# A graph-attention and message-passing kernel: the first four edge groups take keys and values from gathered rows of x, the query table is made first, and table stores and six loads go out on ScalarE's queue

## The reference

```python
q = (x @ Wq.T + bq).reshape(N, H, C)          # N=3125, H=4, C=32
k = (x @ Wk.T + bk).reshape(N, H, C)
v = (x @ Wv.T + bv).reshape(N, H, C)
alpha = jnp.sum(q[dst] * k[src], axis=-1) / np.sqrt(C)
m = jax.ops.segment_max(alpha, dst, num_segments=N)
e = jnp.exp(alpha - m[dst])
z = jax.ops.segment_sum(e, dst, num_segments=N)
msg = (e / z[dst])[:, :, None] * v[src]
out = jax.ops.segment_sum(msg, dst, num_segments=N)
conv = out.reshape(N, H * C) + x @ Wskip.T + bskip
# then: Wout, layer norm, a 512-wide MLP, layer norm: the new node features
# then the second layer: gather of node features by src, a small MLP over the
# edge weights, products with edge directions, segment_sum by dst, W_out, layer norm
```

## Time and profile before

| | us |
|---|---|
| runs (3) | 2982.51, 2999.38, 3002.67; median 2999.38 |
| the profiled execution | 2992.43 |
| its span, first to last instruction | 2990.6 |
| mean granted TensorE clock | 0.728 of full speed |

### The profile page before, as it was taken

One profiled execution on the slowest core, in us unless ns is written; L12 is line 12 of the kernel. 1 busy time (PEld: TensorE's weight loads), 2 busy tenths in 40 slices (PEclk: granted clock), 3 DMA queues, 4 the chain that ended last, 5 costly groups with the idle time before them and its releaser, 6 DMA issues. The chain is left out here.

```text
span 2990.6 us, 37370 instructions
## 1 busy us (share of the span) xinstructions
PE 1866.1 (62%) x9706; PEld 1438.2 (48%) x9706; DVE 1725.1 (58%) x4970; ACT 1264.9 (42%) x3058; POOL 1582.4 (53%) x1617
## 2 busy tenths in 40 slices
PE   3255554554554554545558167877788778777887
PEld 3154443453443444444545045555555555555565
DVE  2454565554554554554666056666666666666678
ACT  0244454554554554544545033433334334333344
POOL 4345555555555555555202756666666666666640
PEclk7556666666666666666678578888887888788889
DMA  7455554544554554544301211111111111111110
GB/s 220 131 144 160 141 139 130 143 135 133 147 140 133 137 147 134 152 129 130 98 2 37 53 37 46 45 46 45 45 46 43 43 45 46 45 44 45 43 33 23
DMA packets 242945, 271.84 MB, mean 91 GB/s; under 512 B 46237, under 2 KB 201971, under 8 KB 242221
## 3 DMA queue, kind: packets, MB, share of 16 engines
q0 software_dynamic: 64480, 158.57, 19.4%
q1 hardware_dynamic: 178252, 110.87, 13.3%
HBM read 257.11 MB, written 12.15 MB: 90 GB/s over the span
## 5 line engine op out<-in xcount | busy, mean ns | idle before, releaser
L476 POOL DMA_INDIRECT rows<-kv_tab,src_col x806 | 770.1, 955 | 688.5 <-DVE msg L1051 436.9
L490 POOL DMA_INDIRECT rows<-up_tab,src_col x806 | 806.5, 1001 | 482.0 <-DVE rows L1359 234.7
L1336 DVE TENSOR_TENSOR acc<-acc,ps 128x256 f32 x808 | 339.2, 420 | 383.3 <-remote 184.6
L709 PE MATMUL ps<-hotT,rows 128*128 128x128 f32 x3232 | 473.9, 308 | 90.5 <-DVE rows L1367 56.7
L709 PEld LDWEIGHTS ps<-hotT,rows 128*128 128x128 f32 x3232 | 463.8, 223 | 127.0 <-DVE rows L1367 80.7
L524 PE MATMUL ps<-qwin,hotT 128*128 128x128 f32 x1616 | 350.5, 381 | 272.0 <-issue 131.9
L535 PE MATMUL ps<-hots,msg 128*128 128x128 f32 x1616 | 353.7, 374 | 210.3 <-issue 172.9
L524 PEld LDWEIGHTS ps<-qwin,hotT 128*128 128x128 f32 x1616 | 314.4, 285 | 310.7 <-issue 232.4
L535 PEld LDWEIGHTS ps<-hots,msg 128*128 128x128 f32 x1616 | 303.4, 274 | 242.0 <-issue 190.0
L1068 DVE TENSOR_TENSOR acc<-acc,ps 128x128 f32 x808 | 227.4, 281 | 254.8 <-remote 193.5
L760 ACT ACTIVATE hotT<-rel,consts 128x512 f32<-128x512 bf16 x202 | 144.7, 716 | 515.3 <-DMA qwin<-q_tab 329.5
(11 more groups left out here) (169 smaller groups left out, 2164.0 us busy)
## 6 DMA issues: line engine op xcount, KB each, us to landing
qwin<-q_tab SPq DMA_DIRECT2D x808, 64.0 KB
rel<-rel_far SPq DMA_DIRECT2D x202, 128.0 KB
rows<-kv_tab,src_col POOLq DMA_INDIRECT x806
rows<-up_tab,src_col POOLq DMA_INDIRECT x806
rows<-emb_rows SPq DMA_DIRECT2D x202, 16.0 KB
weights<-r_far SPq DMA_DIRECT2D x25, 128.0 KB
emb_rows<-weights SPq DMA_DIRECT2D x25, 128.0 KB
kv_tab<-rows SPq DMA_DIRECT2D x12, 256.0 KB, 2.8
```

The source lines that it names most:

```text
L476: nc.gpsimd.indirect_dma_start(kvr[:, q % RING, k, :], None, kv_tab, bass.IndirectOffsetOnAxis(src_col[:, t:t + 1].bitcast(U32), 0)).then_ ...
L490: nc.gpsimd.indirect_dma_start(upr[:, q % RING, k, :], None, up_tab, bass.IndirectOffsetOnAxis(src_col[:, t:t + 1].bitcast(U32), 0)).then_ ...
L709: mm = pe.matmul(ps[:, 4 + 2 * (q % 2) + k // 2, (2 * (k % 2) + m) * P:(2 * (k % 2) + m + 1) * P], left[:, q % 2, k, :], hot2[:, q % 2, k, ...
L1336: v.tensor_tensor(to, to, ps[:, 4 + 2 * (q % 2) + k // 2, (k % 2) * 256:(k % 2) * 256 + 256] .rearrange("p (m f) -> p m f", m=2), ALU.add) ...
```

## The change

Six things.

1. PE and DVE make the query table first, then keys and values; DVE no longer waits for the destination columns ahead of it.
2. The `kv_tab` stores are issued by ACT (after six loads that also move to ACT's queue), the `q_tab` stores stay on SP, now without `kv_tab` ahead of them. The source columns, which POOL needs, are SP's first load.
3. POOL gathers for the groups 0 to 3 (`XQ = 4`) rows of x itself (512 B each, from a new input `x_tab`) before the tables are stored; five pairs of these sixteen gathers wait for steps of DVE's moves. The gathers from `kv_tab` begin with group 4: 790 in place of 806.
4. For these groups PE turns the gathered rows (`x_turned`, four transposes), ACT moves them to SBUF (`x_copied`), PE multiplies with `wqkv` (`x_keys`, four matmuls of 256 columns), DVE adds the bias into the ring place (`x_biased`, two moves of 512 columns).
5. Staging tiles move to the upper half of `rows`, so that the ring places 0 to 11 are free at once; POOL waits for the stores of `q_tab` at group 12, no longer at group 4. ACT's first one-hots wait until the x path is done, since they share `hots`.
6. SP's two small loads (`wskip`, `vecs`) move behind windows 2; the clearing of `acc` moves from slot 2 to slot 9.

```diff
+XQ = 4
-        kv_stage = rowsf[:, 0:8 * QC].rearrange("p (s f) -> p s f", s=8)
-        q_stage = rowsf[:, 8 * QC:15 * QC].rearrange("p (s f) -> p s f", s=7)
+        kv_stage = rowsf[:, 16 * QC:24 * QC].rearrange("p (s f) -> p s f", s=8)
+        q_stage = rowsf[:, 24 * QC:31 * QC].rearrange("p (s f) -> p s f", s=7)
+        xg = acc[:, 1, 0:XQ * QC].rearrange("p (s t f) -> p s t f", s=XQ, t=QT)
+        xgT = hots[:, 0:2 * QC].rearrange("p (b n) -> p b n", b=2)
...
         def _(sp):
+            sp.dma_start(src_col[:], a["src_col"]).then_inc(ld["src"], 16)
...
+            sp.wait_ge(rel_ready, 1)
+            sp.dma_start(rel_far.rearrange("(p n) -> p n", p=P), rel_rows).then_inc(rel_out, 16)
             for g, tiles in enumerate(fours):
                 sp.wait_ge(q_sb, g + 1)
...
         def _(pool):
             pool.wait_ge(ld["src"], 16)
+            for q in range(XQ):
+                for k in range(QT):
+                    t = q * QT + k
+                    if k % 2 == 0 and 1 <= t // 2 <= 3:
+                        pool.wait_ge(q_sb, t)
+                    if k % 2 == 0 and t // 2 >= 4:
+                        pool.wait_ge(kv_sb, 3 * (t // 2) - 11)
+                    nc.gpsimd.indirect_dma_start(
+                        xg[:, q, k, :], None, a["x_tab"],
+                        bass.IndirectOffsetOnAxis(src_col[:, t:t + 1].bitcast(U32), 0)).then_inc(rows_in[q], 16)
             for s in range(8):
                 pool.wait_ge(kv_out[s], 16 * len(range(s, len(pairs), 8)))
-            for q in range(NQ):
-                if q == 4:
+            for q in range(XQ, NQ):
+                if q == 12:
                     pool.wait_ge(q_out, 16 * len(fours))
...
+            def x_turned(g):
+                pe.wait_ge(rows_in[g], 16 * QT)
+                if g:
+                    pe.wait_ge(xt_sb, g)
+                for k in range(QT):
+                    mm = pe.transpose(ps[:, 0, k * P:(k + 1) * P], xg[:, g, k, :], ident)
+                mm.then_inc(xt_mm, 1)
+
+            def x_keys(g):
+                pe.wait_ge(xt_sb, g + 1)
+                if g >= 2:
+                    pe.wait_ge(xkv_sb, 2 * (g - 1))
+                for k in range(QT):
+                    mm = pe.matmul(ps[:, x_banks(g)[k // 2], (k % 2) * 2 * D:(k % 2 + 1) * 2 * D], xgT[:, g % 2, k * P:(k + 1) * P],
+                                   wqkv[:, D:3 * D], start=True, stop=True)
+                mm.then_inc(xkv_mm, 1)
...
+            x_turned(0)
+            x_keys(0)
+            x_turned(1)
             for q in range(-1, LAST_SLOT):
                 b, steps = steps_at(q)
                 if q + 1 < NQ:
                     queries(q + 1)
+                if q + 2 < XQ:
+                    x_keys(q + 2)
+                if q + 3 < XQ:
+                    x_turned(q + 3)
...
         def _(act):
+            act.dma_start(dst_rows, a["dst_rows"]).then_inc(ld["rows"], 16)
...
+            for g, tiles in enumerate(pairs):
+                act.wait_ge(kv_sb, g + 1)
+                act.dma_start(kv_tab[tiles[0] * P:(tiles[-1] + 1) * P, :].rearrange("(t p) f -> p t f", p=P),
...
             def product(q):
                 dve.wait_ge(qe_ready, q + 1)
-                dve.wait_ge(rows_in[q % RING], gathers_to(q))
+                if q < XQ:
+                    dve.wait_ge(xkv_sb, 2 * (q + 1))
+                else:
+                    dve.wait_ge(rows_in[q % RING], gathers_to(q))
...
                     if n == 0 and q < NQ:
                         product(q)
+                    if n == 0 and q + 1 < XQ:
+                        x_biased(q + 1)
```

More of the change, by code:

```diff
@@ L271, in build @@
         hot2 = hotT[:]
-        ld = {k: sem("ld_" + k) for k in ("w", "graph", "const", "src", "r", "attr", "b2", "weights", "lanes", "ends", "dense")}
+        ld = {k: sem("ld_" + k) for k in ("w", "graph", "const", "src", "r", "attr", "b2", "weights", "lanes", "ends", "dense", "rows")}
+        xt_mm, xt_sb, xkv_mm, xkv_sb = sem("xt_mm"), sem("xt_sb"), sem("xkv_mm"), sem("xkv_sb")
         far_in, emb_out = slot_sems("far_in", 2), slot_sems("emb_out", 2)
@@ L364, in _ @@
                              q_stage[:, g, 0:len(tiles) * D].rearrange("p (t f) -> p t f", f=D)).then_inc(q_out, 16)
[L365 to L366 removed]
+            sp.wait_ge(rel_out, 16)
             sp.wait_ge(q_out, 16 * len(fours))
[L368 to L370 removed]
+            sp.wait_ge(ld["graph"], 32)
             def windows(q):
@@ L406, in _ @@
                 windows(q)
+                if q == 2:
+                    sp.dma_start(wskip, a["weights"][:, W_SKIP:W_SKIP + D]).then_inc(ld["w"], 16)
+                    sp.dma_start(vecs[:], a["vecs"]).then_inc(ld["w"], 16)
                 if q == 3:
@@ L497, in _ @@
             pe.wait_ge(ld["w"], 32)
+            landed = 0
+            for g, tiles in enumerate(fours):
+                while landed < 4 and landed * NW // 4 < (tiles[-1] + 1) * P:
+                    pe.wait_ge(ld_x[landed], 16)
+                    landed += 1
+                if g >= 4:
+                    pe.wait_ge(q_sb, g - 3)
+                for k, t in enumerate(tiles):
+                    mm = pe.matmul(ps[:, 4 + g % 4, D * k:D * (k + 1)], xT[:, tile_cols(t)], wqkv[:, 0:D], start=True, stop=True)
+                mm.then_inc(q_mm, 1)
             for g, tiles in enumerate(pairs):
-                for j in range(4):
-                    if tiles[0] == 0 or (tiles[0] * P <= j * NW // 4 < (tiles[-1] + 1) * P):
-                        if j * NW // 4 < (tiles[-1] + 1) * P:
-                            pe.wait_ge(ld_x[j], 16)
                 if g >= 4:
@@ L750, in make_hots @@
             def make_hots(q):
+                if q == 0:
+                    act.wait_ge(rel_ready, 2)
+                    act.wait_ge(xkv_mm, XQ)
                 if q >= HOTS:
@@ L1462, in layout @@
     rows[:N] = f["x"]
+    a["x_tab"] = rows
     a["x_rows"] = rows.reshape(TABLE_TILES, P, D).transpose(1, 0, 2).reshape(P, TABLE_TILES * P)
```

69 lines of the change are left out of this document (34 added, 35 removed).

## The result

| | before | after |
|---|---|---|
| median, 11 runs each on one chip | 2997.43 us | 2988.84 us |
| the profiled execution (its span) | 2992.43 (2990.6) | 2993.15 (2991.3) |
| mean granted TensorE clock | 0.728 | 0.727 |

The ratio is 0.9972 with a 95% interval of 0.9959 to 0.9986: the change takes off 8.4 us (4 to 12), 0.28%. That is within 1%, as forecast, but well short of the 14 us that the sum gave, and 2988.84 lies above the sum's own range of 2970 to 2985. The two profiled executions alone would show nothing: they are 0.7 us apart the other way.

The account below looks back on a forecast made before the run. The attention loop's start, delayed by a slow stretch tied to POOL's unbroken gathers, was taken to bound the kernel. POOL's start at 38, row of 61 and trailing of 5 gave 14 us off 2992.4: 2978 us, range 2957 to 3000.

Parts of the forecast that it names:

- The bound and the carry: Attention loop: its start, POOL's restart at 160.34, sets the time, and any shift of it reaches the end one for one.
- POOL's start, "I take 38 us, bounds 35 and 42": Head: POOL's first gather from `kv_tab` at 38 us, against 27.07 before.
- The sum over bytes: Head: 10.8 MB ahead of the last `kv_tab` store, 37 us at 290 GB/s; windows 0 to 3 up to 5 us more.
- no change on the path: DVE in the head: the same 20 table moves end at 29 to 33 us, 32 taken, so no cost.
- POOL's row, 61 us: POOL after its start: 48 unbroken `kv_tab` gathers at 1.27 us each, ending at 99 instead of 108.4.
- The trailing of 5 us: Behind POOL's last gather of the row: the slow stretch lasts 5 us more (none to 9.2), engines free at 104.
- I take the middle, slot 4 done and slot 5 next: End of the slow stretch: slot 5 next at 104 instead of 121.41, 17 us by that count, 14 us taken.
- rival B: Nothing moves: PE crawls from the first `kv_tab` gather, slot 4 at 115 to 118, gain 0 to 3 us; chance 0.20.
- What the crawl hangs on: Start: while POOL gathers without a break, PE and SP crawl at 0.7 to 1.4 us an instruction; mechanism unknown.
- A: Rival: x path slips through before the crawl, slot 7 at 98 to 104, gain 27 to 33 us; chance 0.30.
- C: Rival, slower: crawl ends with PE's backlog, slot 3 at 160, loop 48 us late, 3040 us; chance 0.08.
- The second queue: Head, `kv_tab` stores on ACT's queue: no bandwidth of its own, worth nothing; otherwise the sum would be 2973.

Follow-up runs that it names:

- late loads: Changed kernel with ScalarE's six loads held until `xT` has landed, relative rows formed behind the query table; ratio 0.9969 to the kernel before.
- POOL held: Changed kernel with POOL's first `kv_tab` gather held until the products of groups 0 to 3 are done; ratio 0.9934 on a crawling chip, 1.0022 on a quiet one.
- stores on SP: Changed kernel with the `kv_tab` stores back on SP's queue, ahead of the windows; ratio 0.9972 to the kernel before.
- no x path: Changed kernel with XQ = 0, all 806 gathers from `kv_tab`, new order kept; ratio 1.0006 on a crawling chip, 1.0052 on a quiet one.
- before, paced: Kernel before with gathers of groups 2 to 15 waiting for the product two groups back; ratio 0.9924 on a crawling chip, 1.0074 on a quiet one.
- paced at the start: Changed kernel with only the gathers of groups 4 to 15 waiting for the product two groups back; ratio 0.9886 to the kernel before.
- both: Changed kernel with gathers of groups 4 to 15 paced and ScalarE's loads held until `xT` has landed; ratio 0.9864 to the kernel before.

## Why the prediction was right and wrong

**The bound and the carry: right.** The time of the crawling chip is set by the moment at which the loop gets going. Restarts are shifted by 5.85 us at 154.49 and by 5.6 at 546.78 (552.40 before), the last product by 4.4.

**POOL's start, "I take 38 us, bounds 35 and 42": wrong, 46.01.** This is the term that was mis-sized, by 8 us and beyond its bound. The sum over bytes was not what failed. The windows 0 to 3 do slip in ahead of the last stores (SP issued them at 27 to 45), which I had left in the upper bound: 12.3 MB instead of 10.8. The quiet chip moved 300 GB/s up to 40 us, at which 12.3 MB take 41 us, and POOL started at 40.01 there, inside the bounds. What failed is the step behind it: the moves of tables on DVE, "no change on the path", with the last at 29 to 33, and the 16 gathers of x hidden "under work that waits for bytes anyway", at no price. On the quiet chip the last move ended at 32.21, as forecast, on the crawling one at 39.33, and without the gathers of x at 32.66. The change brought gathers of POOL into the head, PE slowed beside them, DVE waited for PE, and the stores came late; the rate of 264 to 274 GB/s goes with that. I had tied the crawl to POOL's gathers and not applied it to the new ones.

The shared bandwidth is a smaller part. `xT` now lands 12.1 us after issue (6.7 before) and PE starts at 12.86 and not at 7.65, but DVE's first table move came only 1.0 us later than before (15.02 against 13.99). With the late loads it is at 10.45, and the first gather at 39.22.

**POOL's row, 61 us: right.** 46.01 to 106.18, 60.2 us. **The trailing of 5 us: right here**, 111.21 against 106.18.

**"I take the middle, slot 4 done and slot 5 next": wrong, slot 3 was next.** The crawl set in some 10 us into POOL's row, not 20 as in the old trace: it caught group 2, and the crawling x work of group 3 (bias at 92.31) stood ahead of product 3. The late start is not the reason. With the late loads POOL's row ran from 39.22 to 99.65, the forecast's own 38 to 99, and slot 3 was next all the same (107.17); the restart came at 149.90, 10.4 us early, and the ratio, 0.9969, cannot be told from 0.9972. So a right start would have given 10 us in the traces, and the count of slots was wrong by itself. That is close to rival B, which had slot 4 at 115 to 118 (114.11 measured) and a gain of 0 to 3. What lifted the gain above B's is behind the crawl: slot 3 to the restart took 43.3 us, against 49.1 before (111.22 to 160.34): slot 4 followed 2.9 us behind slot 3 (6.4 before), slot 7 11.1 us behind slot 4 (13.2 before). 14 forecast, 5.9 in the traces, 8.4 by the ratio.

**What the crawl hangs on: right for the start, as far as it went.** I had treated it as tied to POOL's unbroken row without knowing why. Holding the row moves the crawl, and the crawl ends with the row in every kernel (table below). Wrong was to take it as a property of the program: on the quiet chips the same row leaves PE and SP alone. And a price of 1.4 us for each PE instruction is no law: it fits the 22.4 us between queries of 8 matmuls, but PE also stood still from 101 to 129 with one small step in front of it.

**The rivals.** A (27 to 33 us) needed the x path to be through before the crawl. It was not at 46, but the runs with POOL held or paced come near this case, and gave 20 to 40 us. C did not come: the crawl ended with the row, not with PE's backlog.

**The second queue.** The Trainium skill (DMA: Bandwidth & Descriptors, section Issuing engines are not separate DMA queues) had been set against any gain from it. The same stores from SP alone gave the same ratio, 0.9972, which agrees with the rule, though in that run the windows moved behind the stores too.

## What to carry to other kernels

When a kernel has one engine that runs far ahead into a ring, look at what the others do meanwhile: holding it back for a few slots at the start took off 20 to 40 us where it stood idle afterwards anyway, and cost 11 us where it was the bound. A sum over bytes needs all of the traffic that can legally start before the last store, and it gives the end only while the engines that make the bytes keep up: work that is added "in the shadow" has to be priced by what it does to the others (here 6 us on one sort of chip, nothing on the other). A load that is moved to another issuer still takes bandwidth from the load on the path. And a profile of one execution is one chip: before a number is explained by the program, see whether it is there on another chip.

## What the runs showed of the hardware

The same program takes 2245 us on two chips and 2956 to 2998 us on three others, stable within 0.8% on each. The difference lies in stretches in which PE and SP, by the profile, wait for nothing: SP's four loads take 1.88 us or 7 to 14 us, eight small matmuls 1 us or, by the distance of the products, 22. On the crawling chips this begins some 10 to 40 us into a row of POOL's gathers from `kv_tab` and ends a little behind it:

| kernel | POOL's row ends | first quick product | behind it |
|---|---|---|---|
| before | 108.40 | 117.58 (group 4) | 9.2 |
| changed kernel | 106.18 | 111.21 (3) | 5.0 |
| late loads | 99.65 | 107.17 (3) | 7.5 |
| stores on SP | 101.37 | 107.50 (2) | 6.1 |
| no x path | 121.37 | 130.45 (6) | 9.1 |
| POOL held | 123.47 | 132.44 (10) | 9.0 |
| before, paced | 157.08 | 161.31 (15) | 4.2 |
| paced at the start | 150.76 | 154.10 (15) | 3.3 |
| both | 141.72 | 145.14 (15) | 3.4 |

(In the last three it is the row behind the pacing, 28 gathers.)

It costs most in the loop, which keeps its period of 55.5 to 57 us per 8 groups whatever was tried, where POOL alone would need 40.4 (32 gathers at 1.264 us). What in the chip it is, and why a product starts neither with the row nor at a fixed delay from it, stays open: the trace shows no transfer, semaphore or instruction that the standing engines wait for. Slow loading of code is not it as far as the DMA records go: in the kernel before, between 48 and 108, the queues marked "instruction" moved two packets with 0.1% of the DMA engines' time, on the quiet chip six with 0.3%. Every execution here was taken with the profiler's records, so no run shows whether the crawl is there without them.
